# Row maxima of eight heads instead of four per split, eviction and copy, and a new order of the items

## The reference

```python
h = layernorm(x) * (1 + scale) + shift
q, k, v = h @ Wq, h @ Wk, h @ Wv           # 16 heads of 8
attn = softmax(q @ k.T / sqrt(8))          # rope on q and k in layers 1 and 2
x = x + gate * (attn @ v @ Wo)
x = x + gate * (gelu(layernorm(x) * ... @ W1) @ W2)
```

## Time and profile before

| what | us |
|---|---|
| median of 3 runs (lowest, highest) | 376.14 (375.49, 376.29) |
| the profiled execution, its own time | 374.76 |
| its span, first to last instruction | 372.9 |
| PE busy (share of the span) | 362.0 (97%) |
| DVE busy | 328.1 (88%) |
| ACT busy | 316.3 (85%) |
| POOL busy | 186.8 (50%) |
| mean granted clock of PE | 0.995 |

### The profile page before, as it was taken

How to read it: one execution, slowest core, us unless ns; L and a number is a source line. 1 busy time by engine, 2 the same in 40 slices (tenths; PEclk the granted TensorE clock), 3 DMA queues, 4 the chain that set the end, 5 groups by cost and what they waited for, 6 DMA issues and landing times.

```text
span 372.9 us, 10415 instructions
## 1 busy us (share of the span) xinstructions
PE 362.0 (97%) x3706; PEld 205.7 (55%) x3707; DVE 328.1 (88%) x768; ACT 316.3 (85%) x632; POOL 186.8 (50%) x290
## 2 busy tenths in 40 slices
PE   8999899999999999999999999999999999999987
PEld 3634444546655554555556545464645564456876
DVE  6389999999899989899999899999999999963663
ACT  6304688999999898998999889999989999998784
POOL 5435999676497223784024681205861031104874
PEclk9989999999999999999999999999999999999999
DMA  7810257211004100005000023000041000000002
GB/s 227 237 41 15 58 147 182 75 60 35 2 16 130 32 2 6 0 21 156 3 6 3 0 77 97 4 2 6 2 125 49 2 3 4 3 3 3 1 1 58
DMA packets 17187, 17.64 MB, mean 47 GB/s; under 512 B 2460, under 2 KB 15454, under 8 KB 17120
## 3 DMA queue, kind: packets, MB, share of 16 engines
q1 hardware_dynamic: 15840, 16.19, 15.8%
q10 hardware_dynamic: 1296, 0.79, 0.9%
HBM read 6.62 MB, written 0.52 MB: 19 GB/s over the span
## 4 chain that ended last, share of the span: by engine, by line
PE 65%; DVE 7%; POOL 3%; issue 2%; ACT 1%; DVEq 0%; ACTq 0%; POOLq 0%
PE pv_ps L849 19%; PE max_ps L663 11%; PE exp_ps L672 10%; PE max_ps L796 7%; PE exp_ps L783 6%; DVE mx L1150 5%; PE exp_ps L632 2%; PE max_ps L632 2%; PE exp_ps L718 2%; PE max_ps L653 2%; POOL rstd L1171 1%; PE max_ps L754 1%; PE exp_ps L834 1%; PE exp_ps L653 1%; ACT probs L974 1%
## 5 line engine op out<-in xcount | busy, mean ns | idle before, releaser
L1150 DVE TENSOR_REDUCE mx<-max_ps 128x1 f32<-128x512 f32 x384 | 240.6, 681 | 4.9 <-PE max_ps L663 3.6
L974 ACT ACTIVATE probs<-exp_ps 128x512 f32<-128x512 f32 x384 | 201.0, 603 | 11.5 <-PE exp_ps L672 10.6
L663 PE MATMUL max_ps<-k_stack,q_stack 64*128 64x512 bf16 x384 | 111.6, 385 | 2.4 <-DVE mx L1150 0.8
L849 PE MATMUL pv_ps<-probs,v_ones 128*32 128x256 f32 x1536 | 103.1, 385 | 0.0
L672 PE MATMUL exp_ps<-q_stack,k_stack 64*128 64x256 bf16 x768 | 99.3, 272 | 0.0
L1170 POOL TENSOR_SCALAR var_eps<-mv 128x2 f32<-128x2 f32 (+2 forms) x33 | 6.4, 194 | 146.8 <-DVE mv L1008 146.2
L849 PEld LDWEIGHTS pv_ps<-probs,v_ones 128*32 128x32 f32 x1536 | 43.4, 109 | 32.4 <-issue 9.2
L672 PEld LDWEIGHTS exp_ps<-q_stack,k_stack 64*128 64x128 bf16 x768 | 41.6, 94 | 29.2 <-ACT probs L974 12.5
L663 PEld LDWEIGHTS max_ps<-k_stack,q_stack 64*128 64x128 bf16 x384 | 32.1, 94 | 45.6 <-DVE mx L1150 28.2
L986 ACT ACTIVATE mrows<-exp_ps 8x256 bf16<-8x256 bf16 x48 | 17.4, 364 | 13.6 <-PE exp_ps L834 13.5
L783 PE MATMUL exp_ps<-hT,w 128*128 128x256 f32 x96 | 26.7, 397 | 0.0
(11 more groups left out here) (128 smaller groups left out, 492.5 us busy)
## 6 DMA issues: line engine op xcount, KB each, us to landing
k_stack<-parts SPq DMA_DIRECT2D x36, 128.0 KB, 2.5
q_stack<-parts SPq DMA_DIRECT2D x30, 128.0 KB
w<-in_w_dram SPq DMA_DIRECT2D x4, 448.0 KB, 3.9
w<-in_w_dram SPq DMA_DIRECT2D x4, 256.0 KB, 3.0
w<-in_ada_dram SPq DMA_DIRECT2D x1, 896.0 KB, 5.4
w<-in_rows_dram SPq DMA_DIRECT2D x1, 832.0 KB, 8.8
q_stack<-mrows SPq DMA_DIRECT2D x48, 4.0 KB
x<-in_x_dram SPq DMA_DIRECT2D x2, 256.0 KB, 3.5
```

Source lines behind the costliest of these rows:

```text
L663: return pe.matmul(max_bank(n), half(q_stack, b, pair, j)[:, t * P:(t + 1) * P], half(k_stack, b, pair, j), start=True, stop=True)
L849: mm = pe.matmul(pv_ps[32 * j:32 * j + 32, cols_of(g // 2)], v_ones[:, b, kt, 4 * g + j, :], probs[:, (4 * i + j) % RING_P, cols_of(of_two ...
L974: act.activation(probs[:, tile % RING_P, :], exp_bank(e), ACT.Exp, scale=SCORE_SCALE[hc // 2 // NB]).then_inc(exp_read, 1)
L1150: dve.tensor_reduce(mx[:, G % 2, t, 2 * (pair % 2) + j:2 * (pair % 2) + j + 1], max_bank(n), AX_X, ALU.max, negate=True).then_inc(max_read, 1)
```

## The change

Ten of the twelve half chains (all but the first and the last, `FINE`) have two groups of eight heads instead of four of four, so that there are 2 x 4 + 10 x 2 = 28 groups instead of 48. A coarse group has 16 MAX items, 16 rows instead of 8 in the transposes' output, in the copy to `mrows` and in the DMA, and still two transposes, one copy and one DMA. The split is rewritten: the maxima are written unnegated to `mx` in fp32, a `tensor_reduce` writes the negated bf16 into the upper halves of fp32 words, and a second `tensor_reduce` over two elements takes the place of the `tensor_tensor`; the transposes read the upper halves of the words, bf16 at a step of two. Two `memset`s of 64 and 128 words per partition are added at the start of DVE. The first two MAX items of a group (j = 0 and 1) now wait for the ACT copy of ROWS G-2, and the SPLIT for nothing of it. `ORDER_TEXT` is new: 1264 letters instead of 1304, 20 `S` and 20 `R` fewer, the others as many as before.

```diff
--- before.py
+++ after.py
@@ -70,6 +70,9 @@
 GROUPS = H // 4
 HALF_BEATS = PAIRS * TH
 GROUP_BEATS = HALF_BEATS // GROUPS
+FINE = (0, 2 * LAYERS * NB - 1)
+GROUP_LIST = [(hc, m, n) for hc in range(2 * CHAINS) for n in [GROUP_BEATS if hc in FINE else 2 * GROUP_BEATS] for m in range(0, HALF_BEATS, n)]
+GROUP_OF = {(hc, m + i): G for G, (hc, m, n) in enumerate(GROUP_LIST) for i in range(n)}
 QUADS = HALF_BEATS // 2
 
 
@@ -157,7 +160,7 @@
     table = {
         "E": [("EXP", hc, n, j) for hc in half_jobs for n in range(HALF_BEATS) for j in range(HALVES)],
         "m": [tile + (0,) for tile in tiles], "n": [tile + (1,) for tile in tiles],
-        "S": [("SPLIT", G, 0, 0) for G in range(2 * CHAINS * GROUPS)], "R": [("ROWS", G, 0, 0) for G in range(2 * CHAINS * GROUPS)],
+        "S": [("SPLIT", G, 0, 0) for G in range(len(GROUP_LIST))], "R": [("ROWS", G, 0, 0) for G in range(len(GROUP_LIST))],
         "P": [("PV", i, 0, 0) for i in range(2 * CHAINS * QUADS)], "O": [("OUT", hc, 0, 0) for hc in half_jobs],
         "G": [("OG", hc, WHOLE, 0) for hc in half_jobs], "F": [("FOLD", k, WHOLE, 0) for k in range(NB, CHAINS + NB)],
         "V": [("V", k, WHOLE, 0) for k in range(1, CHAINS)], "Z": [("ZQ", k, WHOLE, 0) for k in range(NB, CHAINS)],
@@ -170,17 +173,16 @@
 
 
 ORDER_TEXT = """
-mnmnnmmnmSnmnRmntnmyASmEEnErEnmtnREEmytEEEnmPEmEnntSmmEEnRVEmDnEntEmnEmEDSPnmEEnEPRmmSEDEEnAnmtPRnDEmEnEPEmEmnEEmESPnEDmEnERDPnE
-ErmnxPOEEmnEESPmEmEnRPmEEnGEEEmPESFEEnmnrPRmEanEEnEmESaEEPRanEmnEEPEmEmEEnPamEnEmEPnOErnEEaSGEmPRmnbamnabaabmbnEEabanEmEnbZbambb
-SmnSabbsmnRbPPEnmnaaabEmaEnmEbESnmERPRmEEEnnbbbEEEmEnPDmmEnaEEPEnbEmEEDmSPEnEEmnRPDnOEmEDEEGmESPEnDcnDEEmRFccVnEmEPEcmnmESEcPnnE
-mRccnmccnmESEcmnEEEmRPEnEEmnPEEEcmnEPmEncEEPSEnmnEEPmOEmcGRSEEnmcdEncddREEnmdEFmPPnEndmEcSddmncddnmEEdEZEdnmEEPmdEEnRPnEdcEmnESE
-mddddREDnEmEdmESPDEnEmEnPRDmEnEDEmPEnEEDmnEEnPOESEDmEnmVGEmEnRSPenEmFEmPRnEmEEnPEmEnEEeEmEnSPmEnEmERPnEmEEEPenEEmePnEEmEnPOmSEnE
-eGmERPEEnmfeeZnmfefSenmfeEnmEfRPennmfffefnEmEfefEEmnSEfneeePRmEefmEnEEnPmESEnffffREmEEemnESPmEEnmEPDRnnEEEmEPnEmEnEPmDODEfDDEDnE
-EGSmEPEngmmEEEnRPSEEmnnEVgEmEEgEnPRmngEEPmnEEmEPESEmEnmEPRnEmEgnEEmPSEEnnEmPORnmgGggmnhgEmSEnhhggmEEEnEPgmEEnRPhgmnEmhggEnEEnmhh
-nmhggShnEmESZhEhnmhERgPRnEEmPhEmEnEmhhnEhhEDDhESmEnEmPRnDEnEmEDPnmEEnEDDSPmEEnEmRPOEnmEEEGEnPimSEEEinmEEEPiRmEnEEnEPEmEEmEniSPEm
-EnmEPRiEnEEmnPEmnEEEnPSmEnEmEPORmniGimniimEEnSiiRnEmEmEEVjnmEEnEiPEmEnEnEPESmnEiEmRiPmnjiSiFnEmEEnRPmnPEmEmEnjSEPEmEEEnPREmEnEmP
-jnmOEEnEPmESEEGnEmEPREnkjmEnEmEPnEEESPREEkEkEPEEEEiEiEPkEEEFjPiPOkjjjGjqlkkjllqqlkjqkklqjlkqllklqqqjqqljljkqklijqlqkklllqjqljlqk
-jqiijjlkqkiqljqqklqlkklk
+tnmnAmmtynyAnmmtnnmmntSnmnmRmnmtSnEnDmEERmtnEnEmVESmEnmDEPEnmREEnEnEPSEmEnmEPnEEEmnREmPnDEmEDEnPDEmmErnSDEEPEmnREnEmPnEEmEmEEnEm
+nrEPOEmEErnmPEnEEEmnPESFnGREEmmExParnmEEnEPEmEEnEamEnnEEEmaEPEmnEnEEPmsnaPmnSPmOnamRGaamnabnmabEEbEEnmbaEnEmEnabPmnmbbSabbnmbbmZ
+EEnamERPEbnaaabEnEmmEbbabnaEbEEEmEnDbPEmnEPEmnEEnEPESDEmmEnRPEEEDmnEFPnDmmEEPODnEEmDEGEEnEmPEnEcESmnmEPRnEnEEcmEcPEEmnEEmVcEnEnm
+cPnmccnmccSnmcEmnEcERPEnEmmEPnEEEmcEPEnmEEnPnmOEcGnEEmcdnSEcddEmnEPEEmEdnEPmnRdccddddmnZddEmEnEEPdmEnEPdmEnmSEcEddddRmnEDEEEmdPn
+DEmEDDnEPEEnmEPEnEmnEVmmEEDnPnOEEDEEmSGPREnmFEEnEPmEnEeEmEnPmEEEnmPnEEEmEmPnEEmnSEPmEeREnmeEEEnPnmEEePOEEEmnEGePnmfenmefefemfnef
+mnmefffZfSnemEEffenEEmnEfPeeEmEnefeREEnmffffEmDEnEnEPEmEmeEnEPSmEfEEnmRPEnmEEEPEnEDmEnPEmFnEEmPnOEEnDEDmDPEmEEnSEGDPREmEEnmVgEnm
+EnPnEEEEmgnEgPEEmnmEPEEEnmgEPEnmEEnSPmEgmnRPnmOgGgmnghnmghhEEEEmnhgnEhmgnmhhghShZEmEnhghnmhEERPmnggghEmnEghnEEEmmhhghEnEEDEmPnmD
+DEEnEPhESnEmEnEPREEmnPEmnEmEPEnEmnDEPDEmEmEDnPOnEmEEEGVSEnmnRPEmEEEnmPmEnEEEnPEmEnmEFPnEEmEinmSEFPEnmEEnRPEmEEmiEnmEEEEniPmEnEmE
+POEnEEmiEPnmEEnEPSinEEEmmPRnmiGiiiEnnEmESjimiEEnRPmEEEEnPmnEEmEPnEimEEESPnEEEnmRPmOEnEijEmnESGEmEEEnPREmkEnEnEEmPEnEEmSEPREEkEjE
+PEEEiEPkEEPEEijiPPOjkiGjjjljkqililjkjklqkqkjqlkkllqllkjljqqqqlqqjjlkiqkjlqkklqllqqjljlkkijqijlkqjiqlkjkklqlkqqlq
 """
 
 
@@ -412,10 +414,9 @@
         var_eps = sb("var_eps", [P, 4, T])
         rstd = sb("rstd", [P, 4, T])
         half = sb("half", [P, 5])
-        mx = sb("mx", [P, 2, TH, 4])
-        mparts = sb("mparts", [P, 2, TH, 4, 2], BF16)
+        mx_of = {n: sb(f"mx{n}", [P, 2, 2, TH, HALVES, 2, n // TH]) for n in (GROUP_BEATS, 2 * GROUP_BEATS)}
         ones_rows = sb("ones_rows", [4, S], BF16)
-        mrows = sb("mrows", [8, 2, HALF], BF16)
+        mrows = sb("mrows", [16, 2, HALF], BF16)
         ang, turns = hid_12[:, 0:2], hid_12[:, 2]
 
         def xhat(slot, t):
@@ -579,10 +580,10 @@
                 name, k, h, c = item
                 if name == "ROWS":
                     G = k
-                    hc, g = G // GROUPS, G % GROUPS
+                    hc, first, pairs = GROUP_LIST[G][0], GROUP_LIST[G][1] // TH, GROUP_LIST[G][2] // TH
                     b = (hc // 2) % NB
                     sp.wait_ge(*read_by_act(item))
-                    sp.dma_start(q_stack[MAX_SLOTS, b, 2 * g:2 * g + 2, cols_of(hc % 2)], mrows[:, G % 2, :]).then_inc(rows_in_stack[G % 2], 16)
+                    sp.dma_start(q_stack[MAX_SLOTS, b, first:first + pairs, cols_of(hc % 2)], mrows[0:4 * pairs, G % 2, :]).then_inc(rows_in_stack[G % 2], 16)
                     background(G)
                 if name == "ZQ":
                     sp.wait_ge(*read_by_act(("EXP", 2 * (k - NB) + 1, HALF_BEATS - 1, 1)))
@@ -804,8 +805,8 @@
                 name, k, h, c = item
                 if name == "EXP":
                     hc, n, j = k, h, c
-                    G = GROUPS * hc + n // GROUP_BEATS
-                    if n % GROUP_BEATS == 0 and j == 0:
+                    G = GROUP_OF[hc, n]
+                    if n == GROUP_LIST[G][1] and j == 0:
                         pe.wait_ge(rows_in_stack[G % 2], 16 * (G // 2 + 1))
                     score_for_exp(hc, n, j, 0)
                     score_for_exp(hc, n, j, 1).then_inc(exp_full, 1)
@@ -831,7 +832,8 @@
                     take_exp(n)
                     out = exp_bank(n).bitcast(BF16)
                     for t in range(TH):
-                        mm = pe.transpose(out[0:8, t * P:(t + 1) * P], mparts[:, G % 2, t].rearrange("p a b -> p (a b)"), ident_bf[:, :])
+                        both_parts = mx_of[GROUP_LIST[G][2]][:, G % 2, 1, t].rearrange("p j part a -> p (j part a)").bitcast(BF16)[:, 1::2]
+                        mm = pe.transpose(out[0:2 * GROUP_LIST[G][2], t * P:(t + 1) * P], both_parts, ident_bf[:, :])
                     mm.then_inc(exp_full, 1)
                 elif name == "PV":
 
@@ -983,7 +985,7 @@
                     act.wait_ge(exp_full, n + 1)
                     if G >= 2:
                         act.wait_ge(rows_in_stack[G % 2], 16 * (G // 2))
-                    act.activation(mrows[:, G % 2, :], exp_bank(n)[0:8].bitcast(BF16)[:, 0:HALF], ACT.Copy).then_inc(exp_read, 1)
+                    act.activation(mrows[0:2 * GROUP_LIST[G][2], G % 2, :], exp_bank(n)[0:2 * GROUP_LIST[G][2]].bitcast(BF16)[:, 0:HALF], ACT.Copy).then_inc(exp_read, 1)
                 else:
                     dense(item)
 
@@ -1120,6 +1122,8 @@
                         dve.wait_ge(max_read, FULL[n])
 
             dve.memset(warm[:, :].bitcast(F32), 0.0).then_inc(first_tile_set, 1)
+            for mx in mx_of.values():
+                dve.memset(mx[:, :, :, :, :, :, :], 0.0)
             dve.memset(half[:, 4:5], 0.0).then_inc(zeros_set, 1)
             dve.memset(half[:, 0:T], -0.5).then_inc(id_ready, 1)
             dve.memset(ones_rows[:, :], 1.0).then_inc(ones_tile_set, 1)
@@ -1132,23 +1136,23 @@
                 if name == "SPLIT":
 
                     G = k
-                    m, pt = mx[:, G % 2].rearrange("p t (a j) -> p t j a", j=HALVES), mparts[:, G % 2]
+                    hc, first, beats = GROUP_LIST[G]
+                    mx, pairs = mx_of[beats], beats // TH
+                    upper = mx[:, G % 2, 1].rearrange("p t j part a -> p (t j) (part a)").bitcast(BF16)[:, :, 1::2]
                     for j in range(HALVES):
-                        dve.wait_ge(*read_by_dve(("MAX", G // GROUPS, GROUP_BEATS * (G % GROUPS) + GROUP_BEATS - 1, j)))
-                    if G >= 2:
-                        dve.wait_ge(*read_by_act(("ROWS", G - 2, 0, 0)))
-                    settle(dve.tensor_reduce(pt[:, :, 1:3, :], m.unsqueeze(4), AX_X, ALU.max))
-
-                    dve.tensor_tensor(pt[:, :, 0::3, :], m, pt[:, :, 1:3, :], ALU.subtract).then_inc(max_split, 1)
+                        dve.wait_ge(*read_by_dve(("MAX", hc, first + beats - 1, j)))
+                    settle(dve.tensor_reduce(upper[:, :, pairs:2 * pairs], mx[:, G % 2, 0, :, :, 1].rearrange("p t j a -> p (t j) a").unsqueeze(3), AX_X, ALU.max, negate=True))
+                    dve.tensor_reduce(mx[:, G % 2, 1, :, :, 0].rearrange("p t j a -> p (t j) a"), mx[:, G % 2, :, :, :, 1].rearrange("p both t j a -> p (t j) a both"),
+                                      AX_X, ALU.add, negate=True).then_inc(max_split, 1)
                 elif name == "MAX":
```

(10 more changed lines are left out.)

## The result

The changed kernel takes **377.78 us** (median of 6 runs, 377.35 to 378.20) beside 375.75 for the kernel before (6 runs, 374.49 to 376.29): a ratio of 1.0059, 95% interval 1.0044 to 1.0075. It is **slower by 2.0 us** (2.2 by the ratio), where 369.0, 7.1 us faster, was forecast. The profiled execution took 377.41 us with a span of 375.4. Executions that lie over 1.5% above the fastest of the same kernel are left out of all ratios: one of `light_dve` (818 us) and two of `old_eight_coarse` (392.0 and 392.3).

What follows compares the result with a forecast made beforehand. The prediction took PE, busy 97% of the span, as where the time passes, with DVE and ACT hardly less loaded. Its terms, 4.2 + 3.1 + 1.8 - 1.0 - 1.0 = 7.1 us off 376.14, gave 369.0 us, range 363.5 to 376.5.

Steps and rivals of the forecast that it cites:

- 20 x 0.21 = 4.2 us: PE: 20 groups go with 40 transposes, each pair priced at 0.21 us of PE's time, 4.2 us gained.
- the middle, 3.1 us: PE's loader idle time ahead of the transposes: gain bounded by 1.5 and 4.7 us, the middle taken, 3.1 us.
- Relief between 0 and 3.6, 1.8 us: What lighter DVE and ACT give PE in the middle stretch: 0 to 3.6 us, 1.8 taken.
- Terms one to three: The gains forecast: PE's transposes 4.2 us, its loader's idle time 3.1, relief from lighter engines 1.8.
- V: Theory named after the result, for the removed work: work of this size was never worth 9 us.
- That is not a cost by itself: Head: the first exponential moves from 32.97 to about 40 us, at no cost since the same items are missing later.
- I take 1.0 us: Head, DVE: maxima wait for the copy of ROWS G-2, two waits of at most 1.25 us, 1.0 us lost.
- Tail 1.0 us: Behind the last EXP: 99 letters instead of 93 and one further table load, 1.0 us lost.
- This is hidden: Row DMAs: at most 0.5 us longer, hidden while enough items stand between `R` and the group's first EXP.
- A: Rival: DVE and ACT set the time, PE only shows it; 366 us, chance 0.18.
- C: Rival: PE held by row DMAs at each coarse group's first EXP; 4.9 us slower, 381 us, chance 0.11.
- B: Rival: gain given back in small pieces, at 0.25 us per coarse group 374 us, at 0.35 no change; chance 0.14.

Runs made afterwards that it cites:

- light_dve: The kernel before without the split's second instruction and the wait between the two, order and grouping untouched: 374.21 us, ratio 0.9955.
- old_eight_coarse: The kernel before's list with the new split, waits at their old places, and eight groups made coarse: 388.4 us, ratio 1.0336.
- wait_back: The changed kernel with the moved wait put back to its old places: 376.40 us, ratio 1.0022 to the kernel before.
- head_old_wait_back: The changed kernel with its list up to the fourth `R` from the kernel before and the waits at their old places: 374.90 us, ratio 0.9976.
- new_then_old: The changed kernel, waits put back, with the old head, new list and coarse groups up to the sixth half chain, then before's list: 376.08 us, ratio 1.0023.
- light_rows: The kernel before with one of two transposes, most of the row copy and the second split instruction left out in all 48 groups: 371.50 us, ratio 0.9885.
- light_act: The kernel before with row copies of 8 instead of 256 columns, nothing else changed: 375.42 us, ratio 0.9989.
- the square: Old or new first half (old head) against old or new second half, old first: 1 and 0.9953 with old first half, 1.0023 and 0.9976 with new.

## Why the prediction was wrong, step by step

The ratios make one account, step by step from the changed kernel to the one before. Each step is between two neighbouring runs, and each is uncertain by 0.6 to 0.9 us:

| step | from, to | costs |
|---|---|---|
| the moved wait | 1.0059, 1.0022 (wait_back) | 1.4 us |
| the head's order | 1.0022, 0.9976 (head_old_wait_back) | 1.7 us |
| second half, order and coarse groups | 0.9976, 1.0023 (new_then_old) | -1.8 us |
| first half behind the head, order, coarse groups and the new split | 1.0023, 1 | 0.9 us |

Together 2.2 us. Without wait and head the change is 0.9 us faster than before, where the sum had 9.1 us of gains ahead of its two costs.

- **"20 x 0.21 = 4.2 us" and "the middle, 3.1 us" (PE's transposes): the term that failed most.** Not the count, the price. The start-to-start time at one place is not what a pair costs. In the middle a pair takes 0.166 us from start to start, not 0.21; a doubled pair adds 0.07 us to PE's busy time; and of that the kernel's time shows 0.03, 0.6 us for 20. The second part, the loader's idle time ahead of them, was put at 3.1 us without a reason for its half: PE's loader still waits 4.8 us for the split after the change, with 28 groups, where it was 3.6 with 48. Adding isn't removing, but even light_rows, with half of 96 transposes gone and 18.7 us less of ACT and DVE besides, gives 4.3 in all.
- **"Relief between 0 and 3.6, 1.8 us".** In kind it was right that the lighter engines would be worth little: light_act nothing that can be told, light_dve 1.7. Terms one to three together were 9.1; light_rows shows 4.3 for about that work. If that carries over, nearly 5 us of the 9.1 were never there (V).
- **"That is not a cost by itself" (the head's order): wrong.** The first exponential starts at 42.1 us, 40 forecast, and from the first to the last start of one it is 297.3 us instead of 305.6, 8 less where 15 were forecast. The head's order costs 1.5 to 1.7 us by head_old_wait_back. The argument was that the same items are missing later. They are, but what they free there is worth less than what they take in the head. That this is because engines wait for each other there anyway is likely, and not shown.
- **"I take 1.0 us" (the moved wait): right in place, too small.** 1.4 us measured in the changed kernel, with its head; 0.3 to 0.4 with the old one. The bound of 1.25 for one wait took one maximum with its fillers, but two maxima of group 2 stand ahead of `R` 0, as the forecast itself said: 2 x 0.60 + 0.28 + 0.37 = 1.85, and the 0.42 us that PE's loader idled ahead of the transposes make it 2.3; the trace shows 2.08. "It costs nothing there" for the coarse half chains held, both waits lie in the head, though not wholly for its reason: the first maximum of group 4 stands one letter ahead of `R` 2 and not 5 maxima behind it, and the trace shows no wait at it.
- **"Tail 1.0 us": right.** +1.2 by the last `OUT`, 33.3 us against 32.0, and 33.4 in wait_back.
- **"This is hidden" (row DMAs).** Two standstills, 1.5 us. The forecast counted letters between `R` and the first EXP, and took 2.9 us from transposes to product. In the two places it was 3.4 us, with 9 and 11 letters between. A letter is no measure of time, and SP's queue counts as well, as old_eight_coarse shows.
- **Transposes at a step of two, wider copies, memsets, weight loads:** 220 ns, 364 ns and nothing to see; right. **Table loads:** 22 instead of 25 in all, 17 instead of 21 between first and last EXP; right.
- **The split's second instruction:** 187 and 173 ns, none over 190; right. In the Trainium skill (SBUF — State Buffer, rules on the shared port pair) the reason is that a `tensor_reduce` doesn't contend with GpSimd's reads on trn2. The durations agree; the contention itself was not tried. It didn't matter for the time: 375.9 against 375.6 us.

**The rivals.** A is refuted: its 8.9 us for DVE and 11.4 for ACT need the time to follow their work, but between first and last `OUT` their shares fell from 93 to 91% and from 94 to 91%, over the span to 85 and 82%, and the time rose. The rule named beside it, of the Trainium skill (Perfetto Trace Analysis, on the most-contended engine), pointed to DVE, and DVE's part alone, 8.9 us less busy in light_dve (328.1 to 319.2), was worth 1.7. C came out on its side, slower, and its mechanism is real, but it accounts for 1.5 us and not for 12. **B is the one that comes nearest**: the gain is given back in small pieces. But B had it in equal pieces for each coarse group, and that is not what the square shows: of the 20 groups that go, ten go in each half, and the second half gains 1.8 us where the first loses 0.9. If light_rows' 4.3 us is what the removed work is worth, half of it in each half of the run, then beside wait and head the new order gives back 4.3 - 0.9 = 3.4 us, some 3 of them in the first half. The 1.2 us of the tail and the 0.66 us of group 14 lie in the second half; of what the first gives back, the waits looked at here name only the 0.87 us of group 4. The 3.4 us and their division are an estimate and not shown by a run.

**What stays open.** What in the first half of the new order costs; whether grouping by itself gives anything, since no list was made for both groupings; why three removals give 4.3 us when two of them, each alone, give 0.4 (within the uncertainty) and 1.7; and how far light_rows' figure carries over to the new list, since the estimate above takes it to.
